# The second FFN's down steps with the weights stationary, in a fused Griffin block and MLP kernel

## The chip, the cores and the metric

The kernel runs on one core of one Trainium2 chip. The metric is the device time of one execution in microseconds. Three runs of the kernel before took 583.77, 583.81 and 584.46 us; the median is 583.81 us.

## The reference

The input is x, 4 sequences of 1024 tokens with 256 features. Two blocks follow each other, each with a residual sum and a layer norm:

```
t   = rmsnorm(x) ; xb = conv4(t @ Wx) ; h = rg_lru(xb) (a scan over time) ; mix = (h * gelu(t @ Wy)) @ Wo
h1  = x + mix ; u = rmsnorm(h1)
ffn = (gelu(u @ Wg) * (u @ Wu)) @ Wd          # 256 -> 1024 -> 256
x1  = layernorm(x + h1 + ffn)
out = layernorm(x1 + relu(x1 @ W1 + b1) @ W2 + b2)   # 256 -> 1024 -> 256, the second FFN
```

Everything is float32. Each product is made of three matmuls on a high and a low part of both operands (hi*hi + lo*hi + hi*lo).

## The kernel before, in words

**Tiling.** The 4096 tokens are cut into 8 chunks of 512. A chunk is held in rows (128 partitions of tokens x 4 token tiles x 256 features) for norms and sums, and transposed (128 partitions of features x 512 tokens) as the operand of products. The hidden width of 1024 is cut into 8 slices of 128, so each FFN of a chunk is 8 units: 64 units r of the first FFN, 64 units w of the second.

**Order.** The program is written out by hand as rounds, on each engine alike: `round_of(r)` with `p, m = divmod(r, 8)`. In round r, TensorE (PE) computes the gate and up steps of unit r, the down step of unit r - 1, and, 11 rounds behind, the second FFN's up step of unit w = r - 11 (`mlp_up`, L767 and following) and down step of unit w - 1 (`mlp_down`, L784 and following). Rounds 14 to 16 do two units w each. In the rounds of a period p the mixing part (Wx, Wa, Wi, Wy, scan, Wo) of chunk n = p + 1 is woven in; the periods p = 2 to 6 have it, the last one, p = 7, has not. In period p the last down step of the second FFN's chunk s = p - 2 falls in round m = 3.

**Two forms of product.** `product` (L473 to L482) has the weights stationary and streams 512 tokens: its result is features x tokens. `product_by_tokens` (L484 to L488) has 128 tokens stationary and streams the 256 columns of the weights: its result has tokens in partitions, as the rows need it. A down step is `product_by_tokens` for each of 4 token tiles, 12 matmuls with 256 columns, into the banks SECOND and SECOND + 1 of PSUM.

**Round m = 4 on VectorE (DVE).** `second_sum(s)` (L1598 to L1604) waits for the last down step and adds both banks of PSUM to rows[s % 2], which holds x1 plus b2. Then follow `gate_times_up(r)` (L1612), and, in the mixing periods, the gates and the scan. `gate_lo` (L1616) and `hidden_lo` (L1621) make the low parts for the down steps. In round m = 6 come `add_mix` (L1556), the sum h1 of chunk n, and the statistics of the output's norm.

**GpSimd (POOL).** `gate_hi(r)` (L2033) makes the high part of a gated unit from what `gate_times_up` gave; DVE's `gate_lo(r)` waits for it, and PE's down step of unit r, which stands in round r + 1, waits for that. In its order round m = 4 has `norm_t`, round m = 5 `gate_hi` and `place_t_diagonal`, round m = 6 `norm_u` (with the root-mean-square, L1936) and `gate_hi`.

**Moves by blocks.** For the chunks 1 to 6 x1 is transposed without PE: DVE transposes 32x32 blocks in place of the whole (L1409, into `normed`), and SyncE (SP) issues 16 DMAs, one for each pair of a block row and a block column, that put the blocks where they belong (`move_block`, L236, each 32 partitions x 2 x 128 elements, 32 KB). `move_t` and `move_u` do the same for two other tiles with 12 DMAs each (4 of `move_u`'s are issued by ScalarE). SP's queue runs in a fixed order: load of x, move_x1, move_t, move_u, store of the output. The tokens of these chunks stand in another order inside a chunk while they are transposed (`in_order`, `by_token`), and the second FFN's relu puts its hidden tokens back by token.

**u.** `norm_u` writes u of chunk n in round m = 6, DVE transposes its blocks, SP and ScalarE (ACT) move them, ACT makes uT_hi (L1012) and PE's first gate step of the next period (L645) waits for it.

Of the kernel before, what the change touches and what calls it, by code (L numbers as in the profile page):

```python
# [28 lines left out]
def griffin_mlp_kernel(nc, x, norm1_w, Wx, Wy, conv_w, conv_b, Wi, Wa, lam, Wo, norm2_w, Wg, Wu, Wd,  # L29
# [14 lines left out]
    with ctx:  # L44
# [3 lines left out]
        def sem(name):  # L48
            return ctx.enter_context(nc.semaphore(name))
# [142 lines left out]
        def h1_squares(c):  # L192
            return c + 2 + min(c, 1)
# [49 lines left out]
        MOVES = len(ALL_BLOCKS) * DMA  # L243
        OFF_MOVES = len(OFF_DIAGONAL) * DMA

        def by_blocks(c):
            return 1 <= c < CHUNKS - 1

# [37 lines left out]
        tT_done = sem("tT_done")  # L286
        t_blocks_ready = sem("t_blocks_ready")
        t_blocks_moved = sem("t_blocks_moved")
        first_tT_ready = [sem(f"first_tT_ready{q}") for q in range(PAIRS)]
        second_tT_ready = [sem(f"second_tT{k}_ready") for k in range(KD)]  # L290
        half_wx_done = sem("half_wx_done")
# [89 lines left out]
        @block.sync  # L381
        def _(sync):
            def load_x(c):
                sync.dma_start(xs[c % 2][:, :, :],
                               x_dram[c:c + 1, :, :, :].rearrange("c p t d -> (c p) t d")
                               ).then_inc(x_loaded[c % 2], DMA)

            def load_first_x(q):
                sync.dma_start(xs[0][:, 2 * q:2 * q + 2, :],
                               x_dram[0:1, :, 2 * q:2 * q + 2, :].rearrange("c p t d -> (c p) t d")  # L390
                               ).then_inc(x0_loaded[q], DMA)

            def load_w(n):
                kt = dram[n].shape[0] // P
                sync.dma_start(raw_of[n].rearrange("p (k n) -> p k n", k=kt),
                               dram[n].rearrange("(k p) n -> p k n", p=P)).then_inc(w_loaded[n], DMA)

            def store_out(c):
                for q in range(PAIRS):
                    sync.wait_ge(out_ready, 4 * c + 2 * q + 2)  # L400
                    at = c * PAIRS + q
                    sync.dma_start(out_dram[at:at + 1, :, :, :].rearrange("c p t d -> (c p) t d"),
                                   rows[c % 2][:, 2 * q:2 * q + 2, :]).then_inc(out_stored[c % 2], DMA)

            def move_t(c):
                sync.wait_ge(t_blocks_ready, KD * (c - BLOCKWISE + 1))
                for i, j in OFF_DIAGONAL:
                    move_block(sync, flat(t_blocks), flat(t_raw), t_blocks_moved, i, j)

            def move_x1(c):  # L410
                sync.wait_ge(x1_blocks_ready, KD * c)
                for i, j in ALL_BLOCKS:
                    move_block(sync, flat(normed), flat(gy), x1_blocks_moved, i, j)

            def move_u(c):

                sync.wait_ge(u_blocks_ready, KD * (c - BLOCKWISE + 1))
                for i, j in OFF_DIAGONAL[ACT_MOVES:]:
                    move_block(sync, flat(u_blocks), flat(u_raw), u_blocks_moved, i, j)

            for q in range(PAIRS):
                load_first_x(q)
            for src, name, n in ((norm1_w, "n1", KD), (conv_b, "cb", KD), (lam, "lam", KD),
                                 (norm2_w, "n2", KD), (b1, "b1", KH)):
                sync.dma_start(vec_rows[VECS[name]:VECS[name] + n, :],
                               src.rearrange("(k p) -> k p", p=P)).then_inc(vecs_loaded, DMA)
            sync.dma_start(vec_rows[VECS["cw"]:VECS["cw"] + TAPS * KD, :],
                           conv_w.rearrange("t (k p) -> (t k) p", p=P)).then_inc(vecs_loaded, DMA)
            load_w("x")
            load_x(1)  # L430
            for n in ("a", "i", "y", "g", "u", "o", "d"):
                load_w(n)
            sync.dma_start(b2_rows[:, :], b2.partition_broadcast(P)).then_inc(b2_loaded, DMA)
            for k, loaded in ((0, w_loaded["1"]), (1, second_w1_loaded)):
                if k == 1:
                    sync.wait_ge(lo_split["u"], pieces["u"])
                sync.dma_start(raw_1[k], dram["1"][k * P:(k + 1) * P, :]).then_inc(loaded, DMA)

            for c in range(2, CHUNKS):

                if c == 2:
                    sync.wait_ge(first_xh_ready, PAIRS)
                else:
                    sync.wait_ge(xh_ready, 2 * (c - 2))
                load_x(c)
                if c == 2:
                    sync.wait_ge(lo_split["d"], pieces["d"])
                    load_w("2")
                if c >= 4:
                    move_x1(c - 3)  # L450
                if c >= BLOCKWISE:
                    move_t(c)
                if c >= 4:
                    move_u(c - 1)
                    store_out(c - 4)
            for c in range(CHUNKS - 4, LAST - 1):
                move_x1(c + 1)
                if c + 3 < LAST:
                    move_u(c + 3)
                store_out(c)  # L460
            store_out(LAST - 1)
            for tiles in (slice(0, 2), slice(2, 3), slice(3, 4)):
                sync.wait_ge(out_ready, TT * LAST + tiles.stop)
                at = LAST * PAIRS + tiles.start // 2
                cols = slice(tiles.start % 2, (tiles.stop - 1) % 2 + 1)
                sync.dma_start(out_dram[at:at + 1, :, cols, :].rearrange("c p t d -> (c p) t d"),
                               rows[LAST % 2][:, tiles, :]).then_inc(out_stored[LAST % 2], DMA)
            for i in range(2):
                sync.wait_ge(out_stored[i], (CHUNKS // 2 * PAIRS + i) * DMA)

        @block.tensor
        def _(pe):
# [11 lines left out]
            def product_by_tokens(dst, n, k, hi, lo, start, stop):  # L484

                nc.tensor.matmul(dst, hi, w_hi[n][:, k, :], start=start, stop=False, skip_group_check=True)  # L486
                nc.tensor.matmul(dst, hi, w_lo[n][:, k, :], start=False, stop=False, skip_group_check=True)  # L487
                return nc.tensor.matmul(dst, lo, w_hi[n][:, k, :], start=False, stop=stop, skip_group_check=True)  # L488

            def transposed(src, done, bank=MIX):  # L490
                for f in range(KD):
# [292 lines left out]
            def mlp_down(w):  # L784
                c, m = divmod(w, KH)
                pe.wait_ge(hid_lo_ready, w + 1)
                if m == 0 and c >= 1:
                    pe.wait_ge(s2_ready, 2 * c)
                for tt in range(TT):
                    last = product_by_tokens(half_bank(SECOND, tt), "2", m, hid_hi[:, w % SLOTS, toks(tt)],  # L790
                                             hid_lo[:, w % SLOTS, toks(tt)], m == 0 and tt % 2 == 0, m == KH - 1)
                last.then_inc(e_done, 1)

            def units(r):
# [575 lines left out]
        def _(dve):  # L1370
# [182 lines left out]

            def add_mix(c, q, bank=MIX):
                dve.wait_ge(wo_done, 2 * c + q + 1)
                nc.vector.tensor_tensor(pair_of(h1[c % 2], q), psum[bank + q][:, :], pair_of(xs[c % 2], q),  # L1556
                                        ALU.add).then_inc(h1_ready, 1)

# [27 lines left out]
            def first_sum(c):  # L1586
# [7 lines left out]
                for q in range(PAIRS):  # L1594
                    nc.vector.tensor_tensor(pair_of(rows[c % 2], q), psum[DOWN + q][:, :], pair_of(h1[c % 2], q),
                                            ALU.add).then_inc(s1_ready, 1)

            def second_sum(c):  # L1598
                dve.wait_ge(e_done, 8 * c + 8)
                dve.wait_ge(b2_added, 4 * c + 4)  # L1600
                for q in range(PAIRS):
                    total = pair_of(rows[c % 2], q)
                    nc.vector.tensor_tensor(total, psum[SECOND + q][:, :], total,
                                            ALU.add).then_inc(s2_ready, 1)  # L1604

            def gate_times_up(r):
                dve.wait_ge(gelu_ready, r + 1)
# [112 lines left out]
            def round_of(r):  # L1720
# [13 lines left out]
                    if m == 3 and not mixing:  # L1734
                        split_x1_lo(f)
                if m == 4 and second:
                    second_sum(s)
                if m == 5 and mixing and p == 1:
                    scan_both(n)
                if m == (7 if p == 1 else 6) and mixing:  # L1740
# [182 lines left out]
        def _(pool):  # L1923
# [46 lines left out]
            def norm_u(c):  # L1970
# [5 lines left out]
                if by_blocks(c - 2):  # L1976

                    pool.wait_ge(x1_blocks_moved, MOVES * (c - 2))
                pool.wait_ge(rms2_rstd, h1_squares(c))
                for tt in range(TT):  # L1980
                    nc.gpsimd.tensor_scalar(normed[:, tt, :], h1[c % 2][:, tt, :], rstd2[:, tt:tt + 1], 0.0,
# [27 lines left out]
            def ln_scale(c, i, q):  # L2009
# [5 lines left out]
                nc.gpsimd.tensor_tensor(pair_rstd, pair_rstd, minus_half[:, 0:2],  # L2015
                                        ALU.pow).then_inc(ln_rstd_ready[i], 1)

            def add_b2(c):
                row = rows[c % 2]
                if by_blocks(c):  # L2020
# [15 lines left out]
            def round_of(r):  # L2036
# [15 lines left out]
                        tail(n)  # L2052
                if mixing and m == (7 if p == 1 else 6):
                    norm_u(n)
                if r < UNITS:
                    gate_hi(r)
                if (r == FROM or m == 5 and p >= 2) and n < LAST:
# [82 lines left out]
```

## Time and profile before

| | |
|---|---|
| median of 3 runs | 583.81 us (583.77 to 584.46) |
| the profiled execution | 584.09 us |
| its span, first to last instruction | 582.3 us |
| mean granted TensorE clock | 0.998 |
| PE busy | 575.0 us, 99% |
| DVE busy | 410.3 us, 70% |
| ACT busy | 313.9 us, 54% |
| POOL busy | 208.5 us, 36% |
| bytes moved by DMA | 22.38 MB |

The span is what the profile covers; the profiled execution's own time is 1.8 us longer. Busy shares are means over the span. A row of a timeline gives the start from the span's beginning, the duration, the engine, the line of the kernel, the operation and, in brackets, how long the engine had been idle and who released it. "x2" is two instructions in one row.

### The profile page before, as it was taken

How to read it: one execution, taken by the hardware profiler on the slowest of the kernel's cores; microseconds unless marked ns; L12 is line 12 of the kernel's file. 1: busy time of each engine (PE TensorE's matmuls, PEld its weight loads, DVE VectorE, ACT ScalarE, POOL GpSimd, SP SyncE). 2: the span in 40 equal slices, each digit the busy share in tenths (PEclk: the TensorE clock that was granted, in tenths of full speed). 3: DMA queues.
4: the chain of work that ended last, by engine and by line, in shares of the span. 5: the costliest groups of instructions: out<-in, count | busy, mean ns of one | idle time of the engine just before them, and what ended most of it. 6: DMA issues, size and time to landing. Idle time of an engine off the chain costs nothing.

```text
span 582.3 us, 9342 instructions
## 1 busy us (share of the span) xinstructions
PE 575.0 (99%) x3409; PEld 508.5 (87%) x3409; DVE 410.3 (70%) x737; ACT 313.9 (54%) x600; POOL 208.5 (36%) x318
## 2 busy tenths in 40 slices
PE   8999999999999999999999999999999999999996
PEld 7768888898888988889888988889898898888996
DVE  5889858867747779486885869658795757454665
ACT  6977765844538336483446643575443833232453
POOL 2111335274242543327333354523624043132130
PEclk9999999999999999999999999999999999999999
DMA  7410310011100131002210012100110001100111
GB/s 271 155 37 8 103 36 2 2 27 37 30 7 1 33 95 29 10 1 53 77 37 0 12 43 77 34 1 23 51 33 23 2 1 37 36 1 1 37 37 38
DMA packets 29438, 22.38 MB, mean 38 GB/s; under 512 B 3896, under 2 KB 28624, under 8 KB 29392
## 3 DMA queue, kind: packets, MB, share of 16 engines
q1 hardware_dynamic: 28112, 21.26, 12.0%
q10 hardware_dynamic: 1280, 0.53, 0.4%
q8 instruction: 27, 0.44, 0.3%
q14 instruction: 19, 0.16, 0.1%
HBM read 10.89 MB, written 4.19 MB: 26 GB/s over the span
## 4 chain that ended last, share of the span: by engine, by line
PE 90%; DVE 4%; POOL 2%; ACT 1%; DMA 1%; issue 1%; SPq 1%; DVEq 0%; POOLq 0%; ACTq 0%
PE psum L475 17%; PE psum L477 17%; PE psum L476 17%; PE psum L486 11%; PE psum L488 11%; PE psum L487 11%; PE psum L566 2%; DMA raw_xyai<-in_L_attn_Wi_dram 1%; PE psum L531 1%; PE psum L712 1%; PE psum L714 1%; PE psum L710 1%; DVE gu_lo L1616 1%; PE psum L593 1%; POOL row L2026 0%
## 5 line engine op out<-in xcount | busy, mean ns | idle before, releaser
L2033 POOL TENSOR_SCALAR gu_hi<-gu_raw 128x512 fp32r<-128x512 f32 x64 | 53.9, 842 | 230.3 <-DVE gu_raw L1612 230.2
L1154 ACT ACTIVATE hid_raw<-psum,vecs 128x512 f32<-128x512 f32 x56 | 38.6, 690 | 117.8 <-PE psum L477 117.7
L1612 DVE TENSOR_TENSOR gu_raw<-psum,gu_raw 128x512 f32<-128x512 f32 x64 | 43.8, 685 | 51.6 <-PE psum L477 42.4
L486 PE MATMUL psum<-w_hi,hid_hi 128*128 128x256 f32 x256 | 72.0, 281 | 0.4 <-DVE hid_lo L1621 0.4
L486 PE MATMUL psum<-w_d_hi,gu_hi 128*128 128x256 f32 x256 | 71.9, 281 | 0.0
L488 PE MATMUL psum<-w_hi,hid_lo 128*128 128x256 f32 x256 | 71.9, 281 | 0.0
L488 PE MATMUL psum<-w_d_hi,gu_lo 128*128 128x256 f32 x256 | 71.9, 281 | 0.0
L487 PE MATMUL psum<-w_lo,hid_hi 128*128 128x256 f32 x256 | 71.8, 280 | 0.0
L487 PE MATMUL psum<-w_d_lo,gu_hi 128*128 128x256 f32 x256 | 71.7, 280 | 0.0
L1139 ACT ACTIVATE gu_raw<-psum 128x512 f32<-128x512 f32 x64 | 38.3, 598 | 61.6 <-PE psum L477 36.2
L1616 DVE TENSOR_TENSOR gu_lo<-gu_raw,gu_hi 128x512 fp32r<-128x512 f32 x64 | 47.8, 748 | 24.2 <-POOL gu_hi L2033 24.2
L1621 DVE TENSOR_TENSOR hid_lo<-hid_raw,hid_hi 128x512 fp32r<-128x512 f32 x56 | 41.5, 740 | 32.7 <-ACT hid_hi L1158 32.4
L486 PEld LDWEIGHTS psum<-w_hi,hid_hi 128*128 128x128 f32 x256 | 48.2, 188 | 3.3 <-DVE hid_lo L1621 1.3
L486 PEld LDWEIGHTS psum<-w_d_hi,gu_hi 128*128 128x128 f32 x256 | 48.2, 188 | 3.2 <-DVE gu_lo L1616 0.7
L475 PE MATMUL psum<-uT_hi,w_u_hi 128*128 128x512 f32 x128 | 50.1, 391 | 0.1
L487 PEld LDWEIGHTS psum<-w_d_lo,gu_hi 128*128 128x128 f32 x256 | 48.1, 188 | 2.3
L477 PE MATMUL psum<-uT_hi,w_u_lo 128*128 128x512 f32 x128 | 49.9, 390 | 0.0
L487 PEld LDWEIGHTS psum<-w_lo,hid_hi 128*128 128x128 f32 x256 | 48.1, 188 | 2.1
L476 PE MATMUL psum<-uT_lo,w_u_hi 128*128 128x512 f32 x128 | 49.9, 390 | 0.0
L488 PEld LDWEIGHTS psum<-w_hi,hid_lo 128*128 128x128 f32 x256 | 48.2, 188 | 0.0
L488 PEld LDWEIGHTS psum<-w_d_hi,gu_lo 128*128 128x128 f32 x256 | 48.2, 188 | 0.0
L475 PE MATMUL psum<-uT_hi,w_g_hi 128*128 128x512 f32 x118 | 46.6, 395 | 0.0
(250 smaller groups left out, 1548.2 us busy)
## 6 DMA issues: line engine op xcount, KB each, us to landing
out_dram<-row SPq DMA_DIRECT2D x15, 256.0 KB, 2.2
xs<-in_L_attn_x_dram SPq DMA_DIRECT2D x7, 512.0 KB, 3.5
gy<-normed SPq DMA_DIRECT2D x96, 32.0 KB, 1.9
t_raw<-t_blocks SPq DMA_DIRECT2D x60, 32.0 KB, 1.9
raw_gud<-in_L_attn_Wg_dram SPq DMA_DIRECT2D x1, 1024.0 KB, 9.1
raw_gud<-in_L_attn_Wu_dram SPq DMA_DIRECT2D x1, 1024.0 KB, 11.2
raw_gud<-in_L_attn_Wd_dram SPq DMA_DIRECT2D x1, 1024.0 KB, 13.6
raw_gud<-in_L_ffn_W_dram SPq DMA_DIRECT2D x1, 1024.0 KB, 6.8
```

Of the source, the lines that this page charges most:

```text
L475: nc.tensor.matmul(dst, w_hi[n][:, k, cols], hi[:, k, :], start=(k == 0), stop=False)
L476: nc.tensor.matmul(dst, w_hi[n][:, k, cols], lo[:, k, :], start=False, stop=False)
L477: return nc.tensor.matmul(dst, w_lo[n][:, k, cols], hi[:, k, :], start=False, stop=(k == KD - 1))
L486: nc.tensor.matmul(dst, hi, w_hi[n][:, k, :], start=start, stop=False, skip_group_check=True)
L487: nc.tensor.matmul(dst, hi, w_lo[n][:, k, :], start=False, stop=False, skip_group_check=True)
L488: return nc.tensor.matmul(dst, lo, w_hi[n][:, k, :], start=False, stop=stop, skip_group_check=True)
L1139: nc.scalar.activation(dst, gate, ACT.Gelu_apprx_tanh).then_inc(gelu_ready, 1)
L1154: nc.scalar.activation(raw, hidden, ACT.Relu, bias=vec("b1", m)).then_inc(relu_ready, 1)
L1612: nc.vector.tensor_tensor(gu, up, gu, ALU.mult).then_inc(gu_ready, 1)
L1616: nc.vector.tensor_tensor(gu_lo[:, r % SLOTS, :], gu_raw[:, r % SLOTS, :], gu_hi[:, r % SLOTS, :].bitcast(FP32), ALU.subtract).then_inc(gu ...
L1621: nc.vector.tensor_tensor(hid_lo[:, w % SLOTS, :], hid_raw[:, w % SLOTS, :], hid_hi[:, w % SLOTS, :].bitcast(FP32), ALU.subtract).then_inc ...
L2033: nc.gpsimd.tensor_scalar(gu_hi[:, r % SLOTS, :], gu_raw[:, r % SLOTS, :], 1.0, 0.0, ALU.mult, ALU.add).then_inc(gu_hi_ready, 1)
```

## The change

The down steps of the second FFN for the chunks 0 to 5 (`sum_by_blocks`) use a new form, `product_by_columns`: the weights are stationary, the 512 tokens of the hidden slice stream, and each of the banks SECOND and SECOND + 1 collects 128 features x 512 tokens. A unit has 6 matmuls with 512 columns in place of 12 with 256.

The result then has features in partitions and must come back to rows. In round m = 4 DVE, in place of `second_sum`, transposes the 32x32 blocks of each bank into `normed` (`transpose_e_blocks`); SP issues 16 DMAs (`move_e`) that place them in the half of h1 that is free (`e_rows(c)`, h1[(c + 1) % 2]), each a whole KB of a partition to be read and 8 pieces of 128 bytes to be written, for 32 partitions; and in round m = 5 POOL, ahead of `gate_hi`, adds them to rows (`add_e`, two additions of 128x512). Chunks 6 and 7 stay as they were. Waits are added where the tiles are shared: `add_mix` waits for `add_e` of the chunk three before, `norm_u` for the blocks moved, `move_e` for the first sum that reads the half of h1, the transposes for x1's blocks moved out of `normed`, and the first down step of the next chunk for the transposes in place of the sums.

```
+        def sum_by_blocks(c):
+            return c < CHUNKS - 2
+
+        def e_rows(c):
+            return h1[(c + 1) % 2]
...
+            def move_e(c):
+                sync.wait_ge(e_blocks_ready, KD * (c + 1))
+                sync.wait_ge(s1_ready, 2 * (c + 2))
+
+                blocks = flat(normed).rearrange("p (i g a) -> p i g a", i=GROUPS, a=BLOCK)
+                placed = flat(e_rows(c)).rearrange("p (g j a) -> p g j a", j=GROUPS, a=BLOCK)
+                for i, j in ALL_BLOCKS:
+                    rows_in = slice(j * BLOCK, (j + 1) * BLOCK)
+                    rows_out = slice(i * BLOCK, (i + 1) * BLOCK)
+                    sync.dma_start(placed[rows_out, :, j, :], blocks[rows_in, i, :, :]).then_inc(e_blocks_moved, DMA)
...
                 if c >= 4:
                     move_x1(c - 3)
+                    move_e(c - 4)
...
             for c in range(CHUNKS - 4, LAST - 1):
                 move_x1(c + 1)
+                move_e(c)
...
+            def product_by_columns(n, m, hi, lo):
+
+                for f in range(KD):
+                    cols, dst = slice(f * P, (f + 1) * P), psum[SECOND + f][:, :]
+                    nc.tensor.matmul(dst, w_hi[n][:, m, cols], hi, start=(m == 0), stop=False)
+                    nc.tensor.matmul(dst, w_lo[n][:, m, cols], hi, start=False, stop=False)
+                    last = nc.tensor.matmul(dst, w_hi[n][:, m, cols], lo, start=False, stop=(m == KH - 1))
+                return last
...
                 if m == 0 and c >= 1:
-                    pe.wait_ge(s2_ready, 2 * c)
-                for tt in range(TT):
...
+                    pe.wait_ge(e_blocks_ready, KD * c)
+                if sum_by_blocks(c):
+                    last = product_by_columns("2", m, hid_hi[:, w % SLOTS, :], hid_lo[:, w % SLOTS, :])
+                else:
+                    for tt in range(TT):
...
             def add_mix(c, q, bank=MIX):
                 dve.wait_ge(wo_done, 2 * c + q + 1)
+                if c >= 3:
+
+                    dve.wait_ge(s2_ready, 2 * (c - 2))
...
+            def transpose_e_blocks(c):
+                dve.wait_ge(e_done, 8 * c + 8)
+
+                dve.wait_ge(x1_blocks_moved, MOVES * (c + 1))
+                blocks = flat(normed).rearrange("p (i t k a) -> p i t k a", i=GROUPS, t=TT, k=KD)
+                for f in range(KD):
+                    nc.vector.transpose(blocks[:, :, :, f, :],
+                                        psum[SECOND + f][:, :].rearrange("p (t i s) -> p i t s", t=TT, i=GROUPS)
+                                        ).then_inc(e_blocks_ready, 1)
...
                 if m == 4 and second:
-                    second_sum(s)
+                    transpose_e_blocks(s)
...
+                if c >= 3:
+
+                    pool.wait_ge(e_blocks_moved, MOVES * (c - 2))
...
+            def add_e(c):
+                pool.wait_ge(e_blocks_moved, MOVES * (c + 1))
+                pool.wait_ge(b2_added, 4 * c + 4)
+                for q in range(PAIRS):
+                    total = pair_of(rows[c % 2], q)
+                    nc.gpsimd.tensor_tensor(total, total, pair_of(e_rows(c), q), ALU.add).then_inc(s2_ready, 1)
...
+                if m == 5 and second:
+                    add_e(s)
                 if r < UNITS:
                     gate_hi(r)
```

## Rows read from the trace of the kernel before

**Rows 1.** The page: busy time of the engines, and shares of the chain.

```profile
PE 575.0 (99%) x3409; PEld 508.5 (87%) x3409; DVE 410.3 (70%) x737; ACT 313.9 (54%) x600; POOL 208.5 (36%) x318
...
PE 90%; DVE 4%; POOL 2%; ACT 1%; DMA 1%; issue 1%; SPq 1%; DVEq 0%; POOLq 0%; ACTq 0%
```

**Rows 2.** The waits of PE: us in total, times, longest us.

```profile
PE psum L486 <- DVE hid_lo L1621: 0.4, 2, 0.2
```

**Rows 3.** PE's timeline in the last period: the first matmul of four groups.

```profile
518.81 0.40 PE L475 MATMUL psum<-x1T_hi,w_hi 128*128 128x512 f32 x1
...
520.18 0.28 PE L486 MATMUL psum<-w_hi,hid_hi 128*128 128x256 f32 x1
...
521.59 0.40 PE L475 MATMUL psum<-uT_hi,w_g_hi 128*128 128x512 f32 x1
...
524.32 0.28 PE L486 MATMUL psum<-w_d_hi,gu_hi 128*128 128x256 f32 x1
```

**Rows 4.** Groups by line and form: busy us, mean ns | idle before.

```profile
L1603 DVE TENSOR_TENSOR row<-psum,row 128x512 f32<-128x512 f32 x14 | 9.0, 683 | 0.0
...
L1409 DVE STREAM_TRANSPOSE normed<-row 128x512 f32<-128x512 f32 x12 | 7.8, 690 | 0.6
...
L2007 POOL TENSOR_TENSOR h<-h,xs 128x512 f32<-128x512 f32 x14 | 18.9, 1372 | 17.1 <-DVE uT_lo L1396 16.1 <-ACT normed L1129 1.0
```

**Rows 5.** DMA issues by line (ns min/median/max), landing, and SP's timeline.

```profile
L236 SPq DMA_DIRECT2D gy<-normed x96: 586/597/1367, 150.2 to 507.9; - x96
...
DMA to landing us min/median/max: 1.8/1.9/3.2
...
L402 SPq DMA_DIRECT2D out_dram<-row x14: 372/378/400, 212.7 to 564.9; - x14
...
498.35 10.18 SPq L236 DMA_DIRECT2D gy<-normed  x16
...
330.80 7.62 SPq L236 DMA_DIRECT2D t_raw<-t_blocks  x12
```

**Rows 6.** DMA engines from 293.4 to 304.2 us, one move of x1.

```profile
DMA packets 1196, 0.51 MB, mean 47 GB/s; under 512 B 239, under 2 KB 1195, under 8 KB 1195
...
q1 hardware_dynamic: 1195, 0.49, 18.6%
```

**Rows 7.** Timelines of DVE, POOL and PE in the mixing period p = 4.

```profile
314.86 1.28 DVE L1603 TENSOR_TENSOR row<-psum,row 128x512 f32<-128x512 f32 x2
317.16 0.69 DVE L1612 TENSOR_TENSOR gu_raw<-psum,gu_raw 128x512 f32<-128x512 f32 x1 [1.02 <-PE psum L477]
...
333.80 0.69 DVE L1556 TENSOR_TENSOR h<-psum,xs 128x512 f32<-128x512 f32 x1 [0.75 <-PE psum L488]
...
329.65 0.62 POOL L2033 TENSOR_SCALAR gu_hi<-gu_raw 128x512 fp32r<-128x512 f32 x1 [7.45 <-DVE gu_raw L1612]
...
335.60 0.20 POOL L1936 TENSOR_SCALAR rstd<-ss 128x4 f32<-128x4 f32 x1 [2.27 <-ACT inp L1108]
...
336.35 0.28 PE L486 MATMUL psum<-w_d_hi,gu_hi 128*128 128x256 f32 x1
```

**Rows 8.** Timelines of ACT and PE at the end of that period.

```profile
347.40 1.15 ACT L1012 ACTIVATE uT_hi<-u_raw 128x512 fp32r<-128x512 f32 x2
...
350.18 0.39 PE L645 MATMUL psum<-uT_hi,w_g_hi 128*128 128x512 f32 x1
```

**Rows 9.** Timelines of DVE, POOL and PE in the last period, p = 7.

```profile
516.83 1.28 DVE L1603 TENSOR_TENSOR row<-psum,row 128x512 f32<-128x512 f32 x2
...
528.60 0.70 DVE L1621 TENSOR_TENSOR hid_lo<-hid_raw,hid_hi 128x512 fp32r<-128x512 f32 x1 [1.89 <-ACT hid_hi L1158]
...
525.36 0.62 POOL L2033 TENSOR_SCALAR gu_hi<-gu_raw 128x512 fp32r<-128x512 f32 x1 [5.95 <-DVE gu_raw L1612]
...
531.24 0.28 PE L486 MATMUL psum<-w_d_hi,gu_hi 128*128 128x256 f32 x1
...
534.02 0.28 PE L486 MATMUL psum<-w_hi,hid_hi 128*128 128x256 f32 x1
```

More of the change, by code:

```diff
@@ L288, in griffin_mlp_kernel @@
         t_blocks_moved = sem("t_blocks_moved")
+        e_blocks_ready = sem("e_blocks_ready")
+        e_blocks_moved = sem("e_blocks_moved")
         first_tT_ready = [sem(f"first_tT_ready{q}") for q in range(PAIRS)]
@@ L787, in mlp_down @@
                 if m == 0 and c >= 1:
-                    pe.wait_ge(s2_ready, 2 * c)
-                for tt in range(TT):
-                    last = product_by_tokens(half_bank(SECOND, tt), "2", m, hid_hi[:, w % SLOTS, toks(tt)],
-                                             hid_lo[:, w % SLOTS, toks(tt)], m == 0 and tt % 2 == 0, m == KH - 1)
+                    pe.wait_ge(e_blocks_ready, KD * c)
[3 more added lines that the diff above has]
+                    for tt in range(TT):
+                        last = product_by_tokens(half_bank(SECOND, tt), "2", m, hid_hi[:, w % SLOTS, toks(tt)],
+                                                 hid_lo[:, w % SLOTS, toks(tt)], m == 0 and tt % 2 == 0, m == KH - 1)
                 last.then_inc(e_done, 1)
@@ L1602, in second_sum @@
                     total = pair_of(rows[c % 2], q)
-                    nc.vector.tensor_tensor(total, psum[SECOND + q][:, :], total,
-                                            ALU.add).then_inc(s2_ready, 1)
+                    nc.vector.tensor_tensor(total, psum[SECOND + q][:, :], total, ALU.add).then_inc(s2_ready, 1)
             def gate_times_up(r):
```

## The prediction

> **What bounds the kernel now.** Start with the page's busy shares and the chain that ended last: PE is busy 99% of the span and carries 90% of the chain [rows 1]. The waits of PE's own queue come next: the longest that another engine causes it in the steady part is a fraction of a microsecond [rows 2]. So TensorE's matmuls set the time, and any other engine counts only where it makes PE wait. The group means of the matmuls must not be multiplied, because the records overlap (pipelined, ends modelled); the prices come from start to start in PE's timeline [rows 3]. There, one unit of the second FFN's up step (six matmuls with 512 columns) goes from 518.81 to 520.18, 1.37 us; the down step (twelve with 256 columns) from 520.18 to 521.59, 1.41 us; the next twelve of 512 columns from 521.59 to 524.32, 2.73 us. Two such sixes in one run therefore cost 2.73, one alone 1.37: I read 1.36 for six, and 0.01 once when the form changes from 256 to 512 columns.
>
> **The change part by part.**
>
> *PE.* A down unit of chunks 0 to 5 turns from twelve 256-column matmuls into six 512-column ones with the weights stationary: 1.41 becomes 1.36, and the change of form behind it goes too, 0.01. There are 6 chunks x 8 = 48 units: 48 x 0.06 = 2.9 us, less where mix_out (256 columns) follows: 5 units keep the 0.01. Gain 2.8 us. The halved instruction count buys so little because the 256-column matmul runs at 1.41/12 = 117 ns and the 512-column one at 227 ns: hardly more than the columns themselves. The wait of the next chunk's first down step moves from the sums to the transposes, at the same place of DVE's order.
>
> *DVE.* Two second_sums of 683 ns go, two transposes of 690 ns come, per chunk [rows 4]. No row has a transpose that reads PSUM; the pairs of rows that differ in that alone (sums from PSUM against transposes from SBUF) give 0.69, which I take. Lower bound 0.6, upper twice that, 1.4 each. They stand where the sums stood, before gate_times_up of round m = 4. Cost 0; with mixing DVE idles 1.0 us behind them (its row stands in the group of that period, below), without mixing nothing covers a longer one.
>
> *SP.* New: 16 DMAs per chunk, 96 in all, each 32 KB as the x1 move's, but written in pieces of 128 bytes (256 per DMA, against 64 of 512). An issue of the existing moves takes 597 ns, and with the gap to the next 16 take 10.18 us, 0.64 per issue; the last lands 1.9 us after it is issued [rows 5]. The store, whose DMA has 256 rows of 1 KB, issues in 378 ns [rows 5], so the number of pieces need not lengthen an issue. Bounds: 0.42 per issue (the store's 0.38 and the gap) and, above, 0.92 (the pieces' own time, below). I take 0.64, the row of the same kind (SBUF to SBUF, 32 partitions, 32 KB). What is queued behind move_e on SP: move_t, which in a mixing period begins at 330.80 [rows 5], 4.4 us after move_e would end, then move_u and the stores; none moves.
>
> *The DMA engines.* In the x1 move, 1195 packets take 18.6% of 16 engines in 10.8 us, 27 ns each [rows 6]. A DMA of the new kind puts 16 pieces and one semaphore write on each engine: 17 x 27 = 0.46 us even if a small piece costs as much as a large one, less than the 0.64 of an issue, so the issue sets the pace. The Trainium skill, "DMA: Bandwidth & Descriptors", Specifications, speaks against the change: line rate wants transfers of at least 512 bytes, since smaller ones are read, modified and written. By the row the sum is unchanged; by the rule it would be that of the slow rival below. No row here has data pieces that small.
>
> *POOL.* add_e: two additions 128x512, 1.31 to 1.37 each [rows 4], 2.65 a chunk, put ahead of gate_hi of round m = 5. POOL waits there until all 16 DMAs landed, and behind it queue gate_hi, DVE's gate_lo, hidden_lo, and PE's down step one round later. Both cases must be timed.
>
> Mixing periods (five of them, one shown) [rows 7]: the sums end at 316.14, so SP issues from 316.17, the last at 316.17 + 15 x 0.64 = 325.8, landed 327.7, added by 330.3. gate_hi starts then instead of at 329.65 and ends at 330.9, gate_lo (0.69) at 331.7. PE wants it at 336.35: 4.6 us to spare. The other follower is u: second add_mix at 333.80 finds DVE free at about 332.9, and POOL is free for the root-mean-square at 335.60. uT_hi's first half is done at 348.0 where PE wants it at 350.18 [rows 8], another 2.1 us. DVE's operations beside POOL stretch by some tenths, well inside. Cost 0.
>
> The last period (no mixing, sums of chunk 5) [rows 9]: rounds are short there. Transposes end at 518.11, SP issues from 518.15, the last at 527.75, landed 529.65, added by 532.3. gate_hi, which started at 525.36, ends at 532.9, gate_lo at 533.7. PE wants it at 531.24: a stall of 2.5 us, new, once. DVE is then late too (hidden_lo 528.60 becomes 533.7), but PE needs that 2.8 us after its down step, and the statistics follow before the next gate_times_up; I find no second stall.
>
> **Sum.** -2.8 + 2.5 = -0.3 us. The profiled execution took 584.09 us (span 582.3 and 1.8 around it), 0.28 above the median of the runs, 583.81; the difference goes onto the median: 583.5 us. With P the time per issue, the stall is 2.5 + 15 x (P - 0.64), never under 0; it is gone at P = 0.47. In the mixing periods u is late from P = 0.84 (0.9 us in front of add_mix and 2.1 behind it, over 15), in each of five.
>
> **The rivals.** A measurement can tell about 0.2%, 1.2 us, from no change.
>
> *Cheap issues: faster.* If a source of whole 1 KB rows makes an issue as short as the store's, P = 0.42, nothing stalls and the whole 2.8 stays: 581.0. For: the store's 378 ns with 256 rows. Against: the 96 moves of x1, median 597 ns, none under 586. Anything below P = 0.58 is faster by over 0.2%.
>
> *Slow small pieces: slower.* Place: the 16 DMA engines during move_e. If a 128-byte piece costs over 38 ns, the engines and not the issue pace the move; it decides the sign from P = 0.74 on, 43 ns a piece. At twice the row, 54 ns, P = 0.92: last period 2.5 + 4.2 = 6.7, five mixing periods 15 x 0.08 = 1.2 each, 6, less 2.8: +9.9, 593.7. For: pieces a quarter of the size of any data row here, the same write side 8 rows per partition. Against: of the 1196 packets 239 are under 512 bytes (the moves have no such data: semaphore writes) [rows 6], and the whole mean is 27 ns, so no large fixed cost shows. This is also what the skill's rule above would do.
>
> *Dearer transposes or additions: slower by a little.* If a transpose out of PSUM takes 1.4 instead of 0.69, DVE ends 1.4 later and the last period's stall is 3.9: 584.9. The nearest rows speak against it.
>
> *No gain on PE.* That the weights-stationary form doesn't run at 1.36 would leave only the stall, 586.3; the up step's own rows are exactly this form, so this is unlikely.
>
> **How the numbers follow.** As forecast (P from 0.58 to 0.73): 0.42, within 0.2% almost throughout. Cheap issues 0.29. Slow pieces or issues from 0.74 on 0.21. Dearer transposes 0.05, no gain 0.03. With the edges of the first case (0.04 faster, 0.02 slower), and half of the dearer transposes inside the 0.2%: faster 0.33, within 0.38, slower 0.29. The likeliest case's own range is 582.5 to 585.0. The 8-in-10 range goes from 580.8 (the whole gain) up to 588.5 (P = 0.86 by the formula), leaving out the far part of the slow rival.
>
> **What would show it.** PE: 512-column matmuls at 227 ns under the new line, 1.36 per unit. SP: 16 issues of e in about 10.2 us, 0.60 each; 0.38 would mean the fast rival, over 0.7 the slow one. POOL: in the last period gate_hi of round 61 starting 7 us later than its gu_raw, behind two additions, and PE waiting once some 2.5 us for gate_lo; in mixing periods gate_hi under 1 us late and PE waiting for nothing. DMA engines: about 4100 small packets per move, share under 0.4. The forecast is wrong if PE waits in mixing periods, or if the last period shows no wait at all.

## The result and the profile after

The changed kernel takes 590.53 us (median of 6 runs, 588.3 to 591.49) against 584.13 us of the kernel before in the same runs: a ratio of 1.0106, 95% interval 1.0093 to 1.0119. It is 1.1% slower, where 583.5 was forecast, with a range up to 588.5. The profiled execution took 590.48 us, with a span of 588.2 (before 584.09 and 582.3). So 5.9 of the 6.4 us are in the span; the execution's own time is 2.3 us longer than its span where it was 1.8 before, which is the other 0.5. The traces cover only the span, so nothing here tells what that half microsecond is.

The page of the changed kernel: busy time, TensorE's clock in 40 slices, and the chain by engine.

```profile
PE 577.6 (98%) x3121; PEld 495.7 (84%) x3121; DVE 414.4 (70%) x737; ACT 313.8 (53%) x600; POOL 225.5 (38%) x330
...
PEclk9999999999999999999999999999999999998999
...
PE 86%; issue 5%; DVE 4%; POOL 3%; ACT 1%; SPq 0%; DMA 0%; POOLq 0%; DVEq 0%; ACTq 0%
```

Against [rows 1] PE has 288 matmuls fewer and is busy 2.6 us longer, and one slice of the clock is no longer full. The waits of PE name one that was not there before [rows 2]:

```profile
PE psum L509 <- DVE gu_lo L1664: 3.0, 1, 3.0
```

Where the 5.9 us of span come from is read off marks that fall at the same point of every period: the stores of the output in SP's timeline (start, length).

```profile
212.24 2.03 SPq L412 DMA_DIRECT2D out_dram<-row  x2
...
281.57 1.99 SPq L412 DMA_DIRECT2D out_dram<-row  x2
...
350.93 2.02 SPq L412 DMA_DIRECT2D out_dram<-row  x2
...
487.70 1.03 SPq L412 DMA_DIRECT2D out_dram<-row  x2
...
546.60 24.08 SPq L412 DMA_DIRECT2D out_dram<-row  x4
```

The same stores of the kernel before:

```profile
212.75 2.00 SPq L402 DMA_DIRECT2D out_dram<-row  x2
...
281.88 2.00 SPq L402 DMA_DIRECT2D out_dram<-row  x2
...
487.34 1.02 SPq L402 DMA_DIRECT2D out_dram<-row  x2
...
541.23 24.07 SPq L402 DMA_DIRECT2D out_dram<-row  x4
```

| stretch | before | after | difference |
|---|---|---|---|
| start to the store at 212 | 212.75 | 212.24 | -0.5 |
| one mixing period | 69.13 | 69.33 | +0.20 |
| the four periods from 212 to 487 | 274.59 | 275.46 | +0.9 |
| the last period, between its stores | 53.89 | 58.90 | +5.0 |
| from there to the end | 41.1 | 41.6 | +0.5 |

The start varies by itself: its store stands at 211.9 to 213.6 us in the traces of all the kernels below, so the -0.5 says little. Two things went otherwise than in the sum. The mixing periods were to become up to 0.47 us shorter each (7 units of 0.06 and one of 0.05), and they became 0.20 longer, without any wait of PE. The last period was to lose 2.5 us, and lost 5.0.

**The last period.** DVE, POOL and PE of the changed kernel, in the order of the chain:

```profile
517.54 1.30 DVE L1643 STREAM_TRANSPOSE normed<-psum 128x512 f32<-128x512 f32 x2
...
518.87 10.90 SPq L434 DMA_DIRECT2D h<-normed  x16
...
531.15 2.49 POOL L2074 TENSOR_TENSOR row<-row,h 128x512 f32<-128x512 f32 x2 [11.03 <-DMA h<-normed]
533.62 0.62 POOL L2091 TENSOR_SCALAR gu_hi<-gu_raw 128x512 fp32r<-128x512 f32 x1
...
534.27 0.69 DVE L1664 TENSOR_TENSOR gu_lo<-gu_raw,gu_hi 128x512 fp32r<-128x512 f32 x1 [8.40 <-POOL gu_hi L2091]
...
535.01 0.58 PE L509 MATMUL psum<-w_d_hi,gu_hi 128*128 128x256 f32 x1 [3.03 <-DVE gu_lo L1664]
535.39 0.42 PE L510 MATMUL psum<-w_d_lo,gu_hi 128*128 128x256 f32 x1
```

That is the chain of the prediction [rows 9], link by link: transposes, SP's 16 issues, landing, two additions, gate_hi, gate_lo, and PE waiting 3.03 us. (From start to start it is 3.2 us more than a matmul: the one before begins at 531.60.) What comes behind the wait was not in it. The matmuls after it start 0.21 us apart (0.42 long) instead of 0.118: the granted clock has fallen. Busy time and clock of that stretch, and of the one behind it (us, busy of PE, PEld, DVE, ACT, POOL, then the clock):

```profile
534.50:537.90 3.40, 2.89 (x13) 2.89 (x14) 3.39 (x11) 0.00 (x0) 0.00 (x0) 0.53 0.00 0
538.00:545.00 7.00, 7.00 (x43) 6.17 (x43) 2.08 (x3) 1.87 (x3) 3.31 (x6) 0.99 0.00 1
```

For 3.4 us, from 534.7 to 538.1, the clock stands at 1.2 GHz, half of what was granted before and after. It fell at the end of PE's wait, and PE worked in 3.1 of the 3.4 us. From 535.01 to 538.39 the trace has twelve matmuls of 256 columns and two of 512 in 3.38 us, which cost 1.87 us at their usual 117.5 and 228 ns: 1.5 us are lost. 3.2 + 1.5 = 4.7 of the 5.0. Of the six runs above one, the fastest (588.3 us), had a mean granted clock of 0.999; the five others had 0.995 or 0.996 and took 589.96 to 591.49 us. So the fall did not come in every run, and a run without it is some 2 us shorter.

**The mixing periods.** PE's timeline, an up step, a down step in the new form (L517 to L519) and the first matmuls of the next gate step:

```profile
298.82 0.40 PE L498 MATMUL psum<-x1T_hi,w_hi 128*128 128x512 f32 x1
...
300.19 0.40 PE L517 MATMUL psum<-hid_hi,w_hi 128*128 128x512 f32 x1
300.42 0.40 PE L518 MATMUL psum<-hid_hi,w_lo 128*128 128x512 f32 x1
...
301.60 0.39 PE L498 MATMUL psum<-uT_hi,w_g_hi 128*128 128x512 f32 x1
...
302.99 0.39 PE L498 MATMUL psum<-uT_hi,w_u_hi 128*128 128x512 f32 x1
```

The new unit goes from 300.19 to 301.60: 1.41 us. From the start of one matmul to the start of the next (the pitch) it is 235 ns, and the unit is as long as the twelve by tokens took [rows 3]. And the gate step behind it, with operands that nobody changed, takes 1.39 instead of 1.37. The six matmuls of the up step ahead still take 1.37.

POOL in a mixing period stands nearly as forecast [rows 7]: the additions start at 327.79 (forecast 327.7), but the two take 3.28 us in place of 2.65, and gate_hi is 1.4 us late where under 1 was forecast. PE waits for nothing:

```profile
327.79 3.28 POOL L2074 TENSOR_TENSOR row<-row,h 128x512 f32<-128x512 f32 x2 [5.73 <-DMA h<-normed]
331.05 0.62 POOL L2091 TENSOR_SCALAR gu_hi<-gu_raw 128x512 fp32r<-128x512 f32 x1
```

The move itself, all of it between 315.9 and 327.5 us, and its issues over the whole run (ns min/median/max):

```profile
q1 hardware_dynamic: 4352, 0.53, 26.9%
...
L434 SPq DMA_DIRECT2D h<-normed x96: 585/611/1592, 177.3 to 529.2; - x96
```

4352 packets take 26.9% of 16 engines in 11.6 us: 11.5 ns each, under half of the 27 ns of the x1 move's packets [rows 6]. For the same half MB it is 49.9 us of engine time against 32.1, so a byte is half as dear again, and still the issues set the pace. The Trainium skill ("DMA: Bandwidth & Descriptors", Specifications) says that transfers under 512 bytes are read, modified and written and so miss the full rate. The dearer byte does not contradict that, but no row shows whether this is its mechanism. The same page of the Trainium skill, under "Why small descriptors are slow (HBM only)", says that transfers between SBUF tiles do not suffer the penalty of small descriptors. The 11.5 ns of a packet go with that, the engine time of a byte only in part.

### The profile page after: what moved, and what is told of

It reads as the page before. It is cut to its first block, busy times and chain, and to the rows that moved or that the text cites. A ratio compares the mean times of both kernels' runs of the same rounds, so it can differ in the third digit from the quotient of the medians.

```text
span 588.2 us, 8901 instructions
## 1 busy us (share of the span) xinstructions
PE 577.6 (98%) x3121; PEld 495.7 (84%) x3121; DVE 414.4 (70%) x737; ACT 313.8 (53%) x600; POOL 225.5 (38%) x330
## 4 chain that ended last, share of the span: by engine, by line
PE 86%; issue 5%; DVE 4%; POOL 3%; ACT 1%; SPq 0%; DMA 0%; POOLq 0%; DVEq 0%; ACTq 0%
PE psum L498 16%; PE psum L500 16%; PE psum L499 16%; PE psum L509 7%; PE psum L511 7%; PE psum L510 7%; PE psum L517 4%; PE psum L518 3%; PE psum L519 3%; PE psum L598 2%; POOL row L2084 1%; DVE gu_lo L1664 1%; PE psum L563 1%; PE psum L744 1%; PE psum L746 1%
## 5 line engine op out<-in xcount | busy, mean ns | idle before, releaser
L1669 DVE TENSOR_TENSOR hid_lo<-hid_raw,hid_hi 128x512 fp32r<-128x512 f32 x56 | 41.6, 743 | 30.2 <-ACT hid_hi L1194 29.7
L500 PE MATMUL psum<-uT_hi,w_g_lo 128*128 128x512 f32 x118 | 46.5, 394 | 0.0
L499 PE MATMUL psum<-uT_lo,w_g_hi 128*128 128x512 f32 x118 | 46.4, 393 | 0.0
L498 PE MATMUL psum<-x1T_hi,w_hi 128*128 128x512 f32 x112 | 44.3, 395 | 0.0
L500 PE MATMUL psum<-x1T_hi,w_lo 128*128 128x512 f32 x112 | 43.7, 390 | 0.0
L499 PE MATMUL psum<-x1T_lo,w_hi 128*128 128x512 f32 x112 | 43.7, 390 | 0.0
L517 PE MATMUL psum<-hid_hi,w_hi 128*128 128x512 f32 x96 | 38.3, 399 | 0.4 <-DVE hid_lo L1669 0.3
```

What stands on the lines that cost most here:

```text
L498: nc.tensor.matmul(dst, w_hi[n][:, k, cols], hi[:, k, :], start=(k == 0), stop=False)
L499: nc.tensor.matmul(dst, w_hi[n][:, k, cols], lo[:, k, :], start=False, stop=False)
L500: return nc.tensor.matmul(dst, w_lo[n][:, k, cols], hi[:, k, :], start=False, stop=(k == KD - 1))
L517: nc.tensor.matmul(dst, w_hi[n][:, m, cols], hi, start=(m == 0), stop=False)
L1669: nc.vector.tensor_tensor(hid_lo[:, w % SLOTS, :], hid_raw[:, w % SLOTS, :], hid_hi[:, w % SLOTS, :].bitcast(FP32), ALU.subtract).then_inc ...
```

## The experiments

Two questions were open: is the last period's loss the wait and the clock behind it, and why does the new form give nothing elsewhere? All variants are of the changed kernel unless "the kernel before" is said. The time of one run stands without an interval, and its kernel is compared by its trace; where an interval is given, it is of several runs beside the kernel before.

**1. The additions behind gate_hi in the last period.**

```
-                if m == 5 and second:
+                if m == 5 and second and mixing:
                     add_e(s)
                 if r < UNITS:
                     gate_hi(r)
+                if m == 5 and second and not mixing:
+                    add_e(s)
```

> In the last period alone, POOL's two additions of e stand behind gate_hi of round 61 instead of ahead of it. Theory A (the additions ahead of gate_hi cost the last period a stall of 3.0 us on PE, and the lower TensorE clock that follows it, 3.4 us at half speed, another 1.7): both go, the time falls by 4.5 to 5 us against the changed kernel, to about 585.7, and the granted clock is 0.998 again. Rival B (the clock falls there for another reason, such as the end of the mixing): the stall goes, the clock's fall stays, -3 us. Rival C (the statistics of the output then wait for the additions and make DVE late instead): under -1 us, PE waits in round 62.

Measured: 585.96 us against 583.65, 1.0041 (1.0026 to 1.0055). PE's wait is gone and the clock is full in every slice. POOL and DVE of this kernel:

```profile
526.22 0.62 POOL L2091 TENSOR_SCALAR gu_hi<-gu_raw 128x512 fp32r<-128x512 f32 x1 [5.90 <-DVE gu_raw L1660]
531.69 2.54 POOL L2074 TENSOR_TENSOR row<-row,h 128x512 f32<-128x512 f32 x2 [4.86 <-DMA h<-normed]
...
533.01 0.75 DVE L1604 BATCH_NORM_STATS2 ln_stats<-row 128x6 f32<-128x256 f32 x2 [2.87 <-POOL row L2074]
```

The wait has moved to DVE's statistics, 2.87 us, where PE does not come to wait for DVE. The span fell from 588.2 to 583.7, 4.5 us. That is theory A: wait and clock go together (B would have left the clock's fall, C a wait of PE). The other traces bear it out. The variants of experiments 2 and 3 and the one with 32 bytes in experiment 4 keep a wait of 2.7 to 3.5 us there, and each has one stretch of 3.4 us at 1.2 GHz, which begins between 0.3 us ahead of the wait's end and 1.0 us behind it; the variants without the wait have none before the last matmul. What remains against the kernel before, 1.4 us of span, is in the mixing periods and the end.

**2. The order of the three matmuls.**

```
                     nc.tensor.matmul(dst, w_hi[n][:, m, cols], hi, start=(m == 0), stop=False)
-                    nc.tensor.matmul(dst, w_lo[n][:, m, cols], hi, start=False, stop=False)
-                    last = nc.tensor.matmul(dst, w_hi[n][:, m, cols], lo, start=False, stop=(m == KH - 1))
+                    nc.tensor.matmul(dst, w_hi[n][:, m, cols], lo, start=False, stop=False)
+                    last = nc.tensor.matmul(dst, w_lo[n][:, m, cols], hi, start=False, stop=(m == KH - 1))
```

> The three matmuls of a step of the new form in the order of the other 512-column products: hi*hi, hi*lo, lo*hi (weights' part first). In the changed kernel the new form takes 235 ns a matmul where the others take 227. Theory A (the pitch hangs on the order, because the high part of the weights stands twice in a row): 227 ns, 1.36 us a unit, mixing periods 0.4 to 0.6 us shorter, time -2.8 us. Rival B (it hangs on an operand, not on the order): 235 ns again, time as the changed kernel within 1 us.

Measured: 590.74 us in one run, mixing periods of 69.34 to 69.36 us, a pitch of 235 ns as in the changed kernel. The order does not matter.

**3. A constant tile streamed instead of the hidden units.** The down product of the second FFN for chunks 0 to 5 is not computed in this one.

```
+                    hi, lo = w_hi["g"][:, 0, 0:T], w_lo["g"][:, 0, 0:T]
```

> The new form streams a constant tile (512 columns of Wg's high and low part) instead of the hidden units; the second FFN's down product of chunks 0 to 5 is therefore not computed, everything else runs as before with the same waits. Theory A (the streamed operand, the hidden tiles, is what costs 8 ns a matmul): 227 ns. Rival B (the stationary operand, the accumulating bank or the length of the group is): 235 ns again. Either way the stall of the last period stays, 3 us.

Measured: 586.95 us in one run, with the wait of the last period still there (2.7 us). Groups by line and form (busy us, mean ns), first of the changed kernel, then of this one:

```profile
L517 PE MATMUL psum<-hid_hi,w_hi 128*128 128x512 f32 x96 | 38.3, 399 | 0.4 <-DVE hid_lo L1669 0.3
L518 PE MATMUL psum<-hid_hi,w_lo 128*128 128x512 f32 x96 | 38.3, 399 | 0.0
```

```profile
L518 PE MATMUL psum<-w_g_hi,w_hi 128*128 128x512 f32 x96 | 37.6, 392 | 0.5 <-DVE hid_lo L1670 0.5
L519 PE MATMUL psum<-w_g_hi,w_lo 128*128 128x512 f32 x96 | 37.4, 389 | 0.0
```

The records overlap, so 399 against 389 is not the pitch, but the difference is the same as from start to start: 235 against 227 ns. The gate steps behind are at 227 again too, and a mixing period takes 68.66 us, 0.47 less than before. So it is the streamed operand, and neither the stationary weights, the accumulating bank nor the length of the group. What about that operand, its address or that it is written shortly before, this run does not say. The forecast 0.06 a unit was right for an operand that streams as well as the others do.

**4. The place of the hidden tiles.** What sets the hidden tiles apart from all the others that PE streams is their address. A tile `units_gap` of 96 bytes stands ahead of the gated and the hidden units, so that they begin 96 bytes behind a multiple of 2048, and the others at one (a sum over the sizes of the tiles, in the order of their declaration, counted from the first). The edit puts 32 bytes ahead of the hidden tiles (8 elements); with 24 elements it is 96 bytes, with 232 it is 928. The small tiles declared behind the hidden ones move by as much; experiment 3, which moves no tile, gives the same 227 ns as the best place below.

```
+        sb("hid_gap", [P, 8])
         hid_raw = sb("hid_raw", [P, SLOTS, T])
```

> 32 bytes of padding ahead of the three tiles of the second FFN's hidden units, which otherwise begin 96 bytes behind a multiple of 128. Theory A (the hidden tiles' place in SBUF makes them slow as the streamed operand): with the place a multiple of 128 the new form's matmuls take 227 ns, time -2.8 us. Rival B (the place does not matter): 235 ns again, time within 1 us of the changed kernel.

Measured: 589.64 us in one run; a mixing period of 69.01 us instead of 69.36, and 232 ns a matmul. Half of the loss of a period, so neither of the two answers as put. With the late additions of experiment 1:

> Late additions in the last period and 32 bytes of padding together. If the two effects add (stall and clock: -4.5 us; padding: 0.35 us in each of about six periods), about 584 us, within 0.3% of the kernel before; no wait of PE in the last period; new form 231 ns a matmul.

Measured: 584.46 us against 583.96, 1.0009 (1.0000 to 1.0019). Both effects are there together: no wait of PE in the last period, mixing periods of 69.00 us.

> Late additions, and the hidden tiles 64 bytes behind a multiple of 128 (96 bytes of padding). If the loss grows with the distance from a multiple of 128: between 231 and 235 ns. If only multiples of 128 are good: 235 or more. If 64 bytes are the unit that counts: 231.

Measured: 584.48 us in one run, 233 ns a matmul, a period of 69.11 us. The chunks 6 and 7, whose down steps keep the old form, have 113 ns at some units (two of chunk 6, and those from 559.8 us on), where the kernel before has 117 to 118.

> Late additions, and the hidden tiles padded to a multiple of 1024 bytes (928 bytes of padding), the gated units left where they are. Theory A (place modulo more than 128 matters): under 229 ns a matmul and a time of 582 to 583 us. Theory B (only the place modulo 128 matters): 231 ns, as with 32 bytes, about 584 us.

Measured: 582.57 us in one run, and 227 ns. PE's timeline, the same place in the program as above:

```profile
297.78 0.40 PE L499 MATMUL psum<-x1T_hi,w_hi 128*128 128x512 f32 x1
...
299.14 0.39 PE L518 MATMUL psum<-hid_hi,w_hi 128*128 128x512 f32 x1
...
300.50 0.39 PE L499 MATMUL psum<-uT_hi,w_g_hi 128*128 128x512 f32 x1
...
301.86 0.39 PE L499 MATMUL psum<-uT_hi,w_u_hi 128*128 128x512 f32 x1
```

The down step goes from 299.14 to 300.50, 1.36 us, and so does the gate step behind it. The mixing period takes 68.66 us. Timed:

> The same kernel as e9_pad232, timed: late additions and hidden tiles at a multiple of 1024. From the predicted terms, 2.8 us of gain and no stall, 581 to 582.7 us, faster than the kernel before by 0.2 to 0.5%.

Measured: 582.54 us against 584.03, 0.9975 (0.9966 to 0.9984). This version beats both kernels, by 0.25% and by 1.3%. Of the 2.8 us forecast for PE 1.5 come out in the time: by the trace the four periods are 1.9 us shorter in sum, but from the last stores on the kernel is 0.7 longer, and the 0.5 outside the span stays.

**5. The gap taken out altogether.**

```
-        sb("units_gap", [P, 24])
```

> Late additions, and the 96-byte gap ahead of the unit tiles taken out: the gated units and the hidden units begin at multiples of 2048 bytes like all tiles whose products run at 227 ns. Theory A (a streamed operand wants the place that all the others have): new form 227 ns, 1.36 us a unit. Theory B (128 bytes are enough, the rest of the loss is something else): 231 ns, as with the padding. Either way the 256-column form with units stationary, which had 117 ns before, is expected slower, up to 122 ns as seen for the hidden units with the padding, which for the gated units costs 64 x 12 x 2 to 4 ns, 1.5 to 3 us.

Measured: 585.81 us in one run. The new form runs at 227 ns, its period is 68.98 where it is 68.66 with 928 bytes: what the streamed units win, the gated units, which are the stationary operand of the first FFN's down step, lose again in part, with 119 to 120 ns a matmul instead of 117 to 118. The second FFN's up steps that follow lose too, 232 ns instead of 227. Not all of the 3.2 us between the two runs is this: 1.4 of them are in the start, where PE waits 1.0 us for a load. The 96 bytes are a place for stationary tiles; the change made the hidden ones streamed and left them there.

**6. Is the form or the place worth the time?** The old form at other places, and the combination.

> The kernel before with the 928 bytes of padding that the best version of the new form has. Theory A (the gain of that version comes from the form, at the right place): the old form with its hidden units stationary is slower there, 120 ns against 118, so 584.5 to 585.5. Rival B (the gain comes from the place alone): 582.5.

Measured: the kernel before with 928 bytes of padding ahead of the hidden tiles takes 585.9 us against 584.04, 1.0033 (1.0020 to 1.0045). At that place the old form is slower, with 119 to 120 ns, and the new one faster, so the place alone does not give the gain: it takes the new form at that place. Against the old form at its own place the gain is 1.5 us.

> The kernel before, with the gap ahead of the unit tiles 64 bytes instead of 96, so that gated and hidden units lie 64 bytes behind a multiple of 128. Theory A (a stationary operand 64 bytes behind such a multiple runs the 256-column form at 114 ns, as the hidden units did with 96 bytes of padding): 120 units x 12 x about 3 ns, 4 to 5 us faster than the kernel before, about 579.5. Rival B (the 114 ns came from the hidden units' own place, 192 bytes, and not from its remainder): no change, 583.5 to 584.5.

Measured: 585.48 against 584.03, 1.0027 (1.0016 to 1.0037), slower, which neither answer had. The remainder of 64 is not what made 113 to 114 ns; the 118 of the down steps hardly differ from before, and the products behind them become slower, 230 to 231 ns instead of 228. PE also waits 0.8 us for a load at the start.

> The kernel before with a gap of 192 bytes ahead of the unit tiles instead of 96: gated and hidden units lie 192 bytes behind a multiple of 2048, where the hidden units ran the 256-column form at 114 ns. Theory A (192 bytes is a good place for the stationary operand, whatever tile it is): 120 units x 12 x 3 ns, about 4 us faster than before, 580, so that the new form is not needed for the gain. Rival B (the 114 ns hang on where the hidden units lie against the weights or gated units): 583 to 585.

Measured: 583.87 against 583.8, 1.0001 (0.9991 to 1.0010). No gain.

> The kernel before with 96 bytes of padding ahead of the hidden tiles alone (192 bytes behind a multiple of 2048), the gated units where they were. Theory A (the hidden units' own place, apart from the gated ones', gives the old form its 114 ns): 56 units x 12 x 3 to 4 ns, 2 to 2.7 us faster than before, 581.3 to 582, level with the best of the new form. Rival B: unchanged, 583.5 to 584.2, so that only the streaming form profits from a better place.

Measured: 583.55 against 584.04, 0.9992 (0.9983 to 1.0001). No gain that can be told from none. PE's timeline in the last chunk, the first matmul of a down step and the first one behind it, in this kernel and then in the kernel before:

```profile
561.07 0.28 PE L487 MATMUL psum<-w_hi,hid_hi 128*128 128x256 f32 x1
...
561.75 0.28 PE L711 MATMUL psum<-x1T_hi,w_hi 128*128 128x256 f32 x1
```

```profile
561.33 0.28 PE L486 MATMUL psum<-w_hi,hid_hi 128*128 128x256 f32 x1
...
562.03 0.28 PE L710 MATMUL psum<-x1T_hi,w_hi 128*128 128x256 f32 x1
```

Six matmuls take 0.68 us, 113 ns each, against 0.70. So the 113 to 114 ns do come back in the old form at 192 bytes, from 559.7 us on and at one unit of chunk 6, nearly as with the new form, but from 200 to 540 us all down steps but one run at 117.5 (118.3 once). They hang on something besides the place; what that is stays open.

> The changed kernel with late additions, gated units 64 bytes behind a multiple of 128, hidden units at a multiple of 1024. Theory A: first FFN's down steps at 114 ns (64 units x 12 x 3 ns = 2.3 us), new form at 227: 582.6 - 2.3, about 580.3, so no faster than the kernel before with the smaller gap alone. Rival B: as e9_pad232, 582.6.

Measured: 583.53 against 584.03, 0.9993 (0.9984 to 1.0002).

> The changed kernel with late additions, gated units at 192 bytes behind a multiple of 2048, hidden units at a multiple of 1024. Theory A: the first FFN's down steps at 114 ns, 64 units x 12 x 3 ns = 2.3 us less than the kernel with the padding of 928 bytes, 580.3, level with the kernel before at the same gap. Rival B: 582.5.

Measured: 582.69 against 583.8, 0.9983 (0.9973 to 0.9992). In both the new form runs at 227 ns, and the gated units gain nothing at their new places (118 ns). For the second that is rival B. The first is 0.9 us slower than B's 582.6: with the gated units at 64 bytes the up steps behind them run at 231 ns, as in the kernel before with that gap.

## Why the prediction was wrong, by its own steps

- **What bounds the kernel:** right. PE sets the time, and the other engines matter where it waits.
- **The gain on PE, 2.8 us:** this term failed. Its step was "1.41 becomes 1.36", taken from the up step's rows as "exactly this form". The form was the same, but its streamed operand was not at the same kind of address: 1.41 stayed 1.41, and the step behind it grew by 0.02. With the constant tile (experiment 3) and with the hidden tiles at a multiple of 1024 (experiment 4) the term comes out, 0.47 us a period; of the whole kernel's time it is 1.5 us. "No gain on PE" stood among the rivals at 586.3 with 3 in 100, far too little: the rows showed the hidden tiles only as the stationary operand, and that was a reason to bound the price from both sides.
- **The stall of the last period, 2.5 us:** mechanism and place right, 3.0 measured as PE's idle time, 3.2 from start to start. The 16 issues took 10.90 us in place of 10.2, P = 0.68 (median 611 ns, the longest of all 96 1592), and by the prediction's own formula that is a stall of 3.1. Left out was the clock, a term put at nothing without a reason: PE had 1.2 GHz for 3.4 us around the end of its wait, 1.5 us more. Experiment 1 takes both away together.
- **SP and the DMA engines:** right. 0.61 an issue where 0.60 was taken, so P = 0.65 in the mixing period shown and 0.68 in the last; the small pieces take 11.5 ns, where 27 was the bound, and a move has 4352 packets where about 4100 were forecast. Neither the fast nor the slow rival happened.
- **DVE's transposes out of PSUM:** right, 1.30 us for two, as from SBUF (0.69 each).
- **POOL's additions:** 3.28 us for two beside a busy DVE, 2.49 beside an idle one, where 2.65 was taken; covered in the mixing periods, as forecast, though gate_hi is 1.4 us late there and not under 1.
- **The sum:** a change of -0.3 was forecast, and +6.4 measured (590.53 against 584.13). In the trace the last period lost 5.0 (3.2 for the wait, 1.5 for the clock, 0.3 left over), the mixing periods 0.9, the end 0.5, and the start gained 0.5: 5.9 us of span. The other 0.5 lies outside the span. No term of the sum stood for either of the two halves of a microsecond. The one at the end lies behind the last computation: from DVE's last instruction (below, first of the kernel before, then of the changed one) to the end of the span it is 2.7 us instead of 2.2.

```profile
579.68 0.41 DVE L1647 TENSOR_SCALAR row<-row,ln_mv,ln_rstd 128x256 f32<-128x256 f32 x1
```

```profile
585.05 0.41 DVE L1695 TENSOR_SCALAR row<-row,ln_mv,ln_rstd 128x256 f32<-128x256 f32 x1
```

The last store is issued 0.20 us behind the end of that instruction, and 0.03 in the kernel before; the variants of the new form have 2.5 to 2.9 us from DVE's last instruction to the end, those of the old one 2.2 to 2.3. What makes the difference, nothing here tells.

## What to carry to other kernels

When a tile changes its role from stationary to streamed, the price of the other streamed tiles is only its price if it also lies as they lie; look at where it is allocated, and try one padding before judging the form. A move through DVE, DMA and a third engine needs some 13 us here until the third engine can begin, and 16 until it is done, and it hides only where the engine that closes it has nothing due behind the wait: put the wait behind the work that the bound engine needs next, above all in the periods that are shorter. And a single wait of a few microseconds on an otherwise full TensorE can cost half as much again in its clock, as here in all traces with the wait.

## What the runs showed of the hardware

- A matmul of 128x512 in fp32r has a pitch of 227 ns when its streamed tile (here the hidden units) begins at a multiple of 1024 or 2048 bytes, 232 ns at 128 bytes behind a multiple of 2048, 233 at 192, and 235 at 96. The matmuls behind it, with other operands, are slowed as well, for one or two steps. The 256-column form with the same tiles stationary has 119 to 120 ns at multiples of 1024, 117 to 118 at 96, and at 192 the same in the mixing periods and 113 in the last 18 us of matmuls.
- 128-byte pieces between SBUF tiles take 11.5 ns each on a DMA engine, semaphore writes counted in; the x1 move's packets 27. For the same half MB that is 49.9 us of engine time against 32.1.
- An issue of a DMA with 32 partitions between SBUF tiles takes 0.6 us on SP whether it has 64 or 256 pieces; the store of 256 KB takes 0.38 [rows 5].
- Around the end of a wait of 2.7 to 3.5 us of PE the granted clock was 1.2 GHz for 3.4 us in each of four traces, once; it began 0.3 us ahead of the wait's end in the changed kernel, and 1.0 us behind it in experiment 3. One run of the changed kernel without a trace kept a mean clock of 0.999. The kernel before waits at most 1.5 us (once, at its start) while it has matmuls left, and its clock is full there.
